# Experts 4 and 5 of a routed feed-forward layer: row indices and weights found in one set behind the first up product, routing weights worked out between the sets before

## The reference

```python
x = x + xattn(layernorm(x), ctx_512, Wq, Wkv_expand, Wout)
x = x + ffn(layernorm(x), gate_w, w_gate, w_up, w_down, sw_gate, sw_up, sw_down)
# ffn, T = 1024 tokens, E = 16, K = 4, CAP = 128
scores = softmax(x @ gate_w.T)
topk_w, topk_i = top_k(scores, K)
topk_w = topk_w / (topk_w.sum(-1, keepdims=True) + 1e-20)
rank   = place of each (token, expert) in its expert, in order of token
buf[e, rank]  = token            # the first CAP of each expert
wbuf[e, rank] = topk_w
xg   = xpad[buf]                                        # gather
mid  = silu(xg @ w_gate[e]) * (xg @ w_up[e])
eout = (mid @ w_down[e]) * wbuf[..., None]
y    = zeros.at[buf].add(eout)                          # scatter-add
shared = silu(x @ sw_gate) * (x @ sw_up) @ sw_down
return y + shared
```

## Time and profile before

| | |
|---|---|
| median of 3 executions | 209.1 us (209.04 to 214.68) |
| the profiled execution | 210.42 us, of which the span of the trace is 208.6 |
| busy: PE, DVE, POOL, ACT | 184.7, 126.9, 98.8, 80.3 us |
| mean granted clock of TensorE | 0.989 of full speed |
| HBM over the span | 107 GB/s |

### The profile page before, as it was taken

One profiled execution on the slowest core, in us unless ns is written; L12 is line 12 of the kernel. 1 busy time (PEld: TensorE's weight loads), 2 busy tenths in 40 slices (PEclk: granted clock), 3 DMA queues, 4 the chain that ended last, 5 costly groups with the idle time before them and its releaser, 6 DMA issues.

```text
span 208.6 us, 3921 instructions
## 1 busy us (share of the span) xinstructions
PE 184.7 (88%) x1372; PEld 138.3 (66%) x1372; DVE 126.9 (61%) x359; ACT 80.3 (38%) x173; POOL 98.8 (47%) x130
## 2 busy tenths in 40 slices
PE   7987978989897999899889988989999999999920
PEld 2665745756674876569556766867887788778810
DVE  2683689696689359955585375866676534442043
ACT  3465631755186326541468116121323333331000
POOL 7816998578154104520243000070778888774012
PEclk9999999999999999999999999999999999999995
DMA  5669999991399968413940197851145544454655
GB/s 178 177 123 132 130 128 129 126 135 37 70 340 248 166 189 260 135 50 97 249 166 17 54 261 179 282 181 42 53 77 89 78 73 89 77 61 84 183 201 201
DMA packets 19387, 28.94 MB, mean 139 GB/s; under 512 B 2457, under 2 KB 12681, under 8 KB 19369
## 3 DMA queue, kind: packets, MB, share of 16 engines
q1 hardware_dynamic: 15872, 23.06, 50.1%
q0 software_dynamic: 3184, 5.38, 12.8%
q10 hardware_dynamic: 313, 0.27, 0.4%
HBM read 15.91 MB, written 6.42 MB: 107 GB/s over the span
## 4 chain that ended last, share of the span: by engine, by line
PE 25%; DMA 13%; POOL 11%; issue 10%; DVE 6%; ACT 1%; SPq 0%; POOLq 0%; DVEq 0%; ACTq 0%
DMA odd_d<-y_rows,tok_i 11%; PE s_ps L1489 7%; PE m_ps L1505 4%; PE m_ps L1447 3%; PE o_ps L1409 2%; POOL out L635 2%; DMA xn_t<-odd_d 2%; POOL k_parts L623 2%; POOL xn L623 2%; POOL q_parts L623 2%; DVE top L926 2%; POOL odd_d L635 2%; PE m_ps L1471 2%; PE t_ps L1393 1%; PE m_ps L1424 1%
## 5 line engine op out<-in xcount | busy, mean ns | idle before, releaser
L560 POOL TENSOR_SCALAR_AFFINE_SELECT probs<-probs 128x256 f32<-128x256 f32 (+1 forms) x48 | 23.1, 484 | 42.2 <-ACT probs L703 40.8
L926 DVE TENSOR_REDUCE top<-s_ps 128x2 f32<-128x512 f32 (+1 forms) x48 | 32.1, 685 | 5.4 <-PE s_ps L1359 4.9
L703 ACT ACTIVATE probs<-t_ps 128x512 f32<-128x512 f32 x48 | 27.6, 596 | 8.3 <-PE t_ps L1393 6.0
L1489 PE MATMUL s_ps<-xn_t,sgu 128*128 128x256 f32 (+1 forms) x96 | 23.5, 384 | 0.7 <-DVE s_mid L1011 0.7
L1393 PE MATMUL t_ps<-q_rows,k_rows 128*128 128x256 bf16 (+1 forms) x128 | 19.6, 247 | 1.9 <-ACT probs L703 1.1
L1489 PEld LDWEIGHTS s_ps<-xn_t,sgu 128*128 128x128 f32 (+1 forms) x96 | 16.5, 182 | 3.9 <-DVE s_mid L1011 1.1
L1356 PE MATMUL s_ps<-mask_b,ident_b 128*128 128x256 bf16 (+1 forms) x48 | 15.0, 312 | 4.0 <-DVE top L926 3.6
L1359 PE MATMUL s_ps<-k_rows,q_rows 128*128 128x128 bf16 (+1 forms) x128 | 18.4, 246 | 0.0
L623 POOL DMA_INDIRECT xn<-xn_d,tok_i x4 | 4.2, 1039 | 24.1 <-DVE tok_i L1101 23.2
L1393 PEld LDWEIGHTS t_ps<-q_rows,k_rows 128*128 128x128 bf16 x128 | 10.1, 98 | 6.4 <-ACT probs L703 2.9
L767 ACT ACTIVATE xg_t<-t_ps 128x256 f32<-128x256 f32 x16 | 6.1, 384 | 20.4 <-PE t_ps L1583 20.4
(11 more groups left out here) (193 smaller groups left out, 395.8 us busy)
## 6 DMA issues: line engine op xcount, KB each, us to landing
k_rows<-k_parts SPq DMA_DIRECT2D x24, 128.0 KB, 7.8
q_rows<-q_parts SPq DMA_DIRECT2D x24, 128.0 KB, 7.6
k_rows<-in_w_dn SPq DMA_DIRECT2D x12, 176.0 KB
out<-xs SPq DMA_DIRECT2D x8, 256.0 KB, 3.2
wgu_early<-in_w_gu SPq DMA_DIRECT2D x4, 352.0 KB
q_rows<-in_w_gu SPq DMA_DIRECT2D x4, 352.0 KB
v_ones<-in_w_gu SPq DMA_DIRECT2D x4, 352.0 KB
probs<-in_w_gu SPq DMA_DIRECT2D x4, 352.0 KB
```

The costliest lines, as they stand in the source:

```text
L560: nc.gpsimd.affine_select(out=v, in_=v, compare_op=ALU.is_ge, fill=0.0, base=0, pattern=[[0, v.shape[1]], [1, P]], channel_multiplier=-1). ...
L703: t_ring.emptied(nc.scalar.activation(probs[:, g % 2, u, :], t_ring.bank(job)[:], ACT.Exp, scale=HD ** -0.5), job)
L926: s_ring.emptied(nc.vector.tensor_reduce(dst, src, AX.X, ALU.max), job)
L1489: last = nc.tensor.matmul(s_ring.bank(("gu", b, c))[0:size, S * half:S * half + S], sgu[:, hc, half, at:at + size], xn2_t[:, hc, S * b:S * ...
```

## The change

- `("slots", 2)`, the set with the indices and weights of experts 4 and 5, moves from behind `("weights", 0)` to in front of it: behind the up product of expert 0 and the transposes of expert 1, which themselves move behind that product. The set of experts 6 and 7 now stands ahead of `("weights", 1)` too.
- `("rows", 0)` moves between the two products of the shared expert's first chunk.
- The filling products ahead of `("in", 1)` (four) and ahead of `("weights", 0)` (six) are gone.
- On DVE, `route_weights` is cut in two. Its first six steps stand between the index sets of experts 0, 1 and 2, 3, the last four (`weight_parts`) behind the second set. `shared_out(2)` stands behind the first chunk's `gu_mid`, and the one-hots are made further ahead.
- `slot` is written with its addresses in order, from sources read across; before, the sources were read in order and the result written across.
- ACT copies expert 1's transposed rows behind expert 0's silu. POOL's and SP's programs are the same.

```diff
--- before.py
+++ after.py
@@ -49,10 +49,12 @@
 HOTS = 6
 LEAD = 6
 
-SLOTS_AT = {0: 2, 1: 3, 3: 4, 5: 5, 7: 6, 9: 7}
+SLOTS_AT = {1: 3, 3: 4, 5: 5, 7: 6, 9: 7}
 HOTS_AT = {0: 3, 1: 4, 2: 5, 4: 6, 6: 7}
 
 LATE = 2
+
+EARLY_PAIRS = 2
 Y_BUFS = 5
 SUMS = (("tsum", 0), ("tsum", 1), ("ssum", 2), ("msum", 3))
 
@@ -78,7 +80,7 @@
 )
 
 
-KEEP_BUSY = {("k", 0): 9, ("q", 0): 3, ("x", 1): 2, ("s", 0, 0): 4, ("in", 1): 4, ("weights", 0): 6}
+KEEP_BUSY = {("k", 0): 9, ("q", 0): 3, ("x", 1): 2, ("s", 0, 0): 4}
 
 
 NORM2_STAGES = ("stats 0", "stats 1", "mean", "eps", "guess", *("times v", "times r", "step") * 3, "rows 0", "rows 1")
@@ -125,16 +127,18 @@
             steps.append(("shift", b + 1))
         steps.extend([*fill[1], ("ot", b, 0), ("ot", b, 1), *fill[2], ("at", b), *fill[3], ("wo", b), *fill[4]])
     steps.extend([("x2", B - 1), ("gu", 2, 2), ("logits", B - 1), ("half", 2), ("rank",), ("shared", 2),
-                  ("gate", 3, 0), ("gu", 3, 0), ("rows", 0), ("gate", 3, 1), ("gu", 3, 1), ("rows", 1),
-                  ("gate", 3, 2), ("gu", 3, 2), ("in", 0), ("in", 1)])
+                  ("gate", 3, 0), ("rows", 0), ("gu", 3, 0), ("gate", 3, 1), ("gu", 3, 1), ("rows", 1),
+                  ("gate", 3, 2), ("gu", 3, 2), ("in", 0)])
     for e in range(E):
         steps.append(("up", e))
+        if e == 0:
+            steps.extend([("in", 1), ("slots", EARLY_PAIRS)])
         if e >= 1:
             steps.append(("down", e - 1))
-        if e < 2:
-            steps.append(("weights", e))
         if e in SLOTS_AT:
             steps.append(("slots", SLOTS_AT[e]))
+        if e < EARLY_PAIRS:
+            steps.append(("weights", e))
         if e + 2 < E:
             steps.append(("in", e + 2))
         steps.append(("turn", e))
@@ -637,7 +641,7 @@
                     in_=y_rows[:, e % Y_BUFS, :], in_offset=None, compute_op=ALU.add,
                 ).then_inc(scattered[e % 2], 16)
 
-            for e in range(2 * SLOTS_AT[0] + 2):
+            for e in range(2 * EARLY_PAIRS + 2):
                 gather(e)
             for e in range(E - LATE):
                 scatter(e)
@@ -851,9 +855,10 @@
             for c in range(len(SC)):
                 gu_act(3, c)
             copy_in(0)
-            copy_in(1)
             for e in range(E):
                 act_of(("up", e), P, I, e_act, ACT.Silu, 1.0)
+                if e == 0:
+                    copy_in(1)
                 if e + 2 < E:
                     copy_in(e + 2)
                 copy_turn(e)
@@ -1059,6 +1064,8 @@
                                                     op0=ALU.mult, op1=ALU.add))
                 link(nc.vector.reciprocal(r2[:], r1[:]))
                 link(nc.vector.tensor_tensor(weight[:], weight[:], wide(r2[:], E), ALU.mult))
+
+            def weight_parts():
                 link(nc.vector.tensor_copy(tok_vals[:, :, :, 3], weight[:]))
                 link(nc.vector.tensor_tensor(weight[:], weight[:], tok_vals[:, :, :, 3], ALU.subtract))
                 link(nc.vector.tensor_copy(tok_vals[:, :, :, 4], weight[:]))
@@ -1071,14 +1078,15 @@
                 rank = m_ring.bank(job)[:, 0:NT * E].rearrange("p (t e) -> p t e", t=NT)
                 link(nc.vector.scalar_tensor_tensor(out=kept[:], in0=rank, scalar=float(CAP), in1=chosen[:],
                                                     op0=ALU.is_lt, op1=ALU.mult))
-                m_ring.emptied(nc.vector.scalar_tensor_tensor(out=slot[:].rearrange("p e t -> p t e"), in0=rank, scalar=1.0, in1=kept[:],
-                                                         op0=ALU.add, op1=ALU.mult), job)
+                m_ring.emptied(nc.vector.scalar_tensor_tensor(out=slot[:], in0=rank.rearrange("p t e -> p e t"), scalar=1.0,
+                                                              in1=kept[:].rearrange("p t e -> p e t"),
+                                                              op0=ALU.add, op1=ALU.mult), job)
                 m_ring.wait_emptied(dve, job)
 
             def onehots(e):
                 if e >= HOTS:
                     g = (e - HOTS) // 2
-                    m_ring.wait(dve, ("weights" if g < 2 else "slots", g))
+                    m_ring.wait(dve, ("weights" if g < EARLY_PAIRS else "slots", g))
 
                 nc.vector.tensor_tensor(onehot[:, e % HOTS], slot_iota[:],
                                         slot[:, e, :].unsqueeze(1).to_broadcast([P, CAP, NT]),
@@ -1236,30 +1244,31 @@
             copy_logits(B - 1)
             choose((B - 1,), 2)
             slots_of_tokens()
-            onehots(0)
-            onehots(1)
-            shared_out(2)
-            onehots(2)
+            for e in range(3):
+                onehots(e)
             values_of_slots(("rows", 0), 3)
             rows_of_slots(0)
+            onehots(3)
             gu_mid(3, 0)
-            onehots(3)
+            shared_out(2)
+            route_weights()
             values_of_slots(("rows", 1), 3)
             rows_of_slots(1)
             gu_mid(3, 1)
+            weight_parts()
             onehots(4)
+            onehots(5)
             gu_mid(3, 2)
-            route_weights()
-            onehots(5)
-            early_weights(0)
             for e in range(E):
                 expert_mid(e)
                 if e >= 1:
                     expert_out(e - 1)
-                if e == 1:
-                    early_weights(1)
+                if e == 0:
+                    slots_of(EARLY_PAIRS)
                 if e in SLOTS_AT:
                     slots_of(SLOTS_AT[e])
+                if e < EARLY_PAIRS:
+                    early_weights(e)
                 if e in HOTS_AT:
                     onehots(2 * HOTS_AT[e])
                     onehots(2 * HOTS_AT[e] + 1)
@@ -1556,7 +1565,7 @@
             def slots(job, lo, hi):
 
                 m_ring.begin(pe, job)
-                if job == ("weights", 0):
+                if job == ("slots", EARLY_PAIRS):
                     pe.wait_ge(vals_ready, 1)
                 n = hi - lo
                 for j, e in enumerate((2 * job[1], 2 * job[1] + 1)):
```

## The result

| | before | after |
|---|---|---|
| median, us | 209.79 (15 runs) | 207.63 (15 runs) |
| profiled execution, us | 210.42 | 207.35 |
| its span, us | 208.6 | 205.6 |

The ratio is 0.988, 95% interval 0.985 to 0.992: 2.5 us less (1.8 to 3.2), within the 2% that count as no change here. It is taken without the executions that are over 1.5% above the fastest of their kernel (two of before, four of the changed kernel), so it isn't quite the ratio of the medians. Forecast were 206.8 us and a gain of 2.3. The changed kernel was timed again beside the experiments: ratio 0.983 (0.977 to 0.988), an interval that reaches past the 2%; median 206.27 us, which is 3.7 us less (2.5 to 4.9).

A forecast was written before the change was run, and what follows sets the result against it. Expert 2's scatter was taken as the bound, held by POOL's run and TensorE's rows. Gains of 0.65, 1.5 and 0.2 us made 2.35, rounded to 2.3, off 209.1: 206.8 us (chance 0.55), range 205.6 to 209.0.

The forecast's parts named there:

- The narrow place: At expert 2's scatter: the kernel gains the smaller of POOL's advance and TensorE's advance plus 0.22 us.
- First rows, 0.65: At expert 0's transposes on TensorE: earlier gathered rows let them begin near 139.2 instead of 139.85, gaining 0.65 us.
- The forecast of 0.4 for the new form of `slot`: On DVE behind the ranks: the step takes 0.4 us instead of 0.73, without mattering for the first index products.
- Expert 0's transposes to index products, 1.5: On TensorE: without fillings and with the indices first, index products begin at 141.5, gaining 1.5 us more.
- POOL's slack, 0.2: At expert 2's scatter: POOL, free at 153.5, lets it start at 153.8, adding 0.2 us to TensorE's lead.
- DVE delivers: On DVE before TensorE's index products: expert 5's one-hot is ready about 141.7, wanted at 142.0, fitting by 0.3 us.
- if TensorE waits for one-hots: A sign of being wrong, at the index products near 141.5, which were to start with no wait for DVE.
- Rival 1: Before the index products: late first-gather landing or slow DVE loses part; gain about 1.6 us, 207.5 us; chance 0.22.
- Rival 2: At the last three odd scatters: landings stretch by what POOL gains, leaving no gain, 209.1 us; chance 0.11.
- Rival 4: At POOL's run: the whole 3.2 us of its advance arrives, giving 205.9 us; chance 0.08.
- Rival 3: On TensorE, 139.2 to 146: without fillings the clock falls to 1.2 GHz, costing 6.4 us, 213.2 us; chance 0.04.

The follow-up runs named there:

- e2: The changed kernel with the ten filling products put back at the same two steps; 209.18 us, ratio 1.000 to the kernel before.
- e4: The changed kernel with the first index products again behind the chunk's second half and `shared_out(2)` between the one-hots; 208.58 us (4 runs).
- e5: The changed kernel with only the old form of `slot`, written across, put back; 206.42 us (2 runs), ratio 0.978 to the kernel before.
- e1: The kernel before without its ten filling products and nothing else of the change; 210.91 us against 209.38, ratio 1.003.
- e7: The changed kernel with the one-hots of experts 10 and 11 made one expert later on DVE; 207.43 us (4 runs), ratio 0.983.
- e9: The changed kernel with each one-hot of experts 6 to 15 cut into four instructions of a quarter; 207.59 us, ratio 0.987.
- e10: The changed kernel once more, unaltered, on the same chip beside the same runs of the kernel before; ratio 0.983.
- e6: The changed kernel with four useless pairs of one-hots added on DVE beside experts 5, 7, 8 and 9; too few runs to compare times.
- e8: The changed kernel with two filling products added behind expert 0's transposes, beside ACT's copy; 207.75 us, ratio 0.984.
- e3: The changed kernel with the weights of experts 0 and 1 again ahead of experts 4 and 5's indices; 207.14 us (5 runs), ratio 0.984.

## Why the prediction was right, and where its steps were off

**The narrow place: right.** What counts is what arrives at expert 2's scatter, and from there POOL's run and the landings shift as a whole. After shows 1.91 there and 1.89 at expert 9's scatter; e2 turns it round, since nothing arrives there and nothing is gained, with POOL's early gathers kept.

**First rows, 0.65: the term was mis-sized.** The transposes did come 0.84 earlier, but I counted this on to the end. e4, where the first gather starts as late as before, loses 0.15 at the second up product, and this through DVE's one-hots. Two things behind the first rows stop their lead: expert 4's one-hot, and in other executions the second gather. The forecast of 0.4 for the new form of `slot` (0.37) was good, and that it doesn't matter for the first gather held too (e5).

**Expert 0's transposes to index products, 1.5: it measured 1.98 - 0.84 = 1.14**, as the products started at 141.68, not 141.5, and the transposes at 139.01, not 139.2. By e4, which keeps all but the early rows, this part with its neighbours carries 1.93 - 0.15 = 1.78 of the 1.93 at the second up product. e1 shows what is in it. I spoke of fillings that go; taking them out alone gave 0.24. The rest is two waits which they had covered, 0.50 for the second gather (its rows are now wanted only behind the first up product) and 1.10 for DVE's weights (which DVE now has 2.3 us sooner).

**POOL's slack, 0.2: it did not come.** The step that failed is "is free for expert 1's scatter at 146.9 + 4.55 = 151.45" and then "POOL free at 153.5": the scatter began at 151.89, because expert 0's scatter was at 147.16 instead of 146.9 and the gather at 149.09 took 1.24, and it took 2.09. This gather and this scatter started while a one-hot ran. By the row y2 alone expert 2's scatter would have been at 154.06, and 154.28 is POOL. So the profile gave 1.91 for 2.35: 0.2 is missing on TensorE's side and 0.2 on POOL's. The first timing, 2.5 (1.8 to 3.2), holds both; that it lies so near the forecast of 2.3 is in part luck, as the path gave 1.9. The second, 3.7 (2.5 to 4.9), lies above the 1.9, and what it has beyond it is open.

**DVE delivers: only just.** The weights fit between the index work. But the one-hots were forecast for 141.7 and end at 140.71 + 1.41 = 142.12, so nothing is left of the 0.3 us to spare: the index products at 141.68 begin 0.15 behind expert 4's one-hot. By its own sign ("if TensorE waits for one-hots") the prediction was wrong here, by some 0.1 us: where the one-hot is there in time, as in e5, e7, e9 and e10, the products begin 0.24 behind expert 1's transposes, here 0.35.

**Rival 1** (a late landing, a late DVE) did not occur at the first gather, where TensorE was the later one. It did occur in small at the second, which the prediction did not follow: TensorE waits 0.16 to 0.50 us for it in the five profiles named under e5, though it marks no wait in the first profile of the changed kernel. **Rival 2** (landings that stretch): 3.73, 3.91, 6.80, so no. The last of them is not steady; it is 3.8 in e2, e5, e6 and e8, but there the load behind it takes 7.0 to 7.2 us instead of 4.6, and from expert 9's scatter to the end every profile but that of before needs 26.6 to 27.6 us. **Rival 4** (all 3.2 us) fell at expert 0's scatter, which waits for its row. **Rival 3**, the clock: in after's profile the granted clock is 1.00 from 131 us to the end of the products, as in this window with its short wait:

```profile
139.00:142.00 3.00, 2.43 (x15) 1.38 (x14) 2.90 (x7) 1.19 (x4) 1.90 (x2) 1.00 0.45 106
```

This is one execution; 8 of the changed kernel's 15 have a mean clock under 0.985, as 9 of before's 19 beside e1 do, and without a profile it isn't known where they lose it. The mechanism exists: e1 shows it behind 1.83 of 3.00 busy, and e4 and e5, both the changed kernel with one piece put back, have it at the same place. There it costs 1.5 us at expert 1's scatter (22.83 and 22.80 against 21.29), not the 6.4 for which I priced it, since it is short. The Trainium skill, "TensorE: Matmul & The Clock Gate", section "HAM oscillation — how this bites in real kernels", warns that waits between bursts of products slow the next burst. e1 agrees in kind, with waits of 0.50 and 1.10 us (2.37 us for a product of 1.35 behind them); e4 fell with TensorE shown full, so in these rows a wait just ahead of the fall is not needed. Profiles also show it elsewhere (e3 at 20 to 24 us, e8 at 6 to 12), and what decides between executions of one kernel was not found.

## What to carry to other kernels

A filling product on the critical engine can stand on a wait. Taking it out paid only together with that wait here: alone it gave 0.24 us at the second up product (and behind it the clock fell), with both waits moved 1.9. When one engine comes early, look for what it meets next: here a one-hot and the second gather, so that the first rows' 0.84 us were worth 0.15. Follow a lead to the narrowest place behind it and count what passes there, not what arrives first: POOL was 2.9 us ahead, the end 1.9. And when the order changes, look at what now starts beside what; one scatter that met a one-hot used up the slack that was to be gained.

## What the runs showed of the hardware

An indirect DMA that POOL issues while a one-hot (`tensor_tensor`, both operands in SBUF) runs on DVE is held until about the end of that one instruction. In twelve profiles every gather from 140 us on that took 1.05 us or more, and every scatter of experts 0 to 8 that took over 1.62, started in such an instruction. The extra is what was left of it, less some 0.12 us: 0.27 left gives 1.12 instead of 0.98, 0.40 left 1.25 instead of 0.98, 0.61 left 2.09 instead of 1.60 (ends worked out from a pair's start and duration, the single one taken as 0.69). One that had started before the one-hot is not touched (e6, 166.20).

It is not this operation alone. In before a `tensor_scalar` that makes a one-hot from SBUF at the end goes with the same:

```profile
181.94 0.74 DVE L1144 TENSOR_SCALAR onehot<-rest,tok_f 128x1024 f32<-128x1024 f32 x1
...
182.26 1.88 POOL L635 DMA_INDIRECT out<-y_rows,tok_i  x1 [0.30 <-issue]
```

Expert 10's scatter started 0.42 us before that one's end and took 1.88 instead of 1.59. In e1 the same scatter started 0.30 before the end of a `y_rows`, which reads PSUM, and took its 1.59. Expert 10's scatters of e9 and e10 (1.68 and 1.67) started in no DVE instruction and stay unexplained.

The Trainium skill, "SBUF — State Buffer", section "Who interferes with whom", says that a DVE instruction with two SBUF inputs contends with a GpSimd instruction that reads SBUF; these rows agree, and e9 adds that the unit is the single instruction.
